# Eight-core transformer layer: three PSUM copies of the attention stage issued on ScalarE instead of VectorE

## The chip, the cores and the metric

One Trainium2 chip, 8 cores. Each core computes one batch element (2048 tokens of width 1024) of the same program; nothing is exchanged between cores. The metric is the device time of the slowest core in microseconds. The lines named L... are lines of the kernel file.

## The reference, cut to what matters

```python
x = x + 0.5 * ffn(layernorm(x))      # attention with 8 heads, 8 experts a head, top-2 gates
x = x + lightnet(layernorm(x))       # the stage that is changed
x = x + 0.5 * ffn(layernorm(x))

def lightnet(x):                     # T 2048, H 8 heads of 128
    q = silu(x @ Wq.T); k = x @ Wk.T; v = x @ Wv.T
    z = cumlogsumexp(k, axis=1)      # running over the tokens
    k = exp(k - z); g = shifted(z) - z
    # per token: S = exp(g) * S + k (x) v ;  o = q . S * 128**-0.5
    gate = x @ Wg1.T @ Wg2.T
    o = o * rsqrt(mean(o * o) + EPS) * g_norm_weight
    return (o * gate * sigmoid(gate)) @ Wo.T
```

## The kernel before

The program has three stages one after the other, each with a layer norm ahead of it: the feed-forward block, the recurrent attention ("GLA", `emit_gla`), and the feed-forward block again. Every instruction is put on an engine's stream by a helper that works out, from the buffers read and written, which semaphore counts it must wait for. Each engine runs its own stream strictly in the order in which the generators below emitted it, so that an instruction which waits holds up everything behind it on its engine. Weights come in 256 KB pieces over two staging slots and are cast by POOL.

In `emit_gla` the 8 heads are taken in 4 pairs, head A as s = 0 and head B as s = 1. For a pair:

- `proj_q(s, h, qtr)` projects one quarter (512 tokens) of one head: 8 matmuls for Q into bank 4 + s, Silu on ACT (L578); 8 for K into the same bank, a copy on DVE (L587); 8 for V into the same bank, a copy to SBUF (L597), 4 transposes on PE (L605) into the bf16 bank `PBB[s]`, and a copy of these to `VHB(s)` (L609).
- `fe_gen(s, h, qtr)` turns K and Q of the quarter into their decayed forms: Exp on ACT (L617), a cast on DVE (L620), a running sum on DVE (L627), a carry copy (L630), Ln and Exp on ACT (L633, L636), a multiply on DVE (L641). `fe_pair` does it for both heads, step by step in turn. PE can go on with the next chunk only when L641 is done.
- `chunk(s, h, c)` does 128 tokens of the recurrence with small 128 x 128 matmuls, two DVE operations (L662, L683) and two ACT Identity operations, L670 (out of `PBB[s]`) and L688.

The order for a pair: `proj_q` of quarters 0 and 1 for both heads, `fe_pair(0)`, chunks 0 to 3, `fe_pair(1)`, chunks 4 to 7 with the two `proj_q` of quarter 2 woven in one step a round and what is left of them after chunk 7 (`drain_bg`), `fe_pair(2)`, chunks 8 to 11 with quarter 3 in the same way, `fe_pair(3)`, chunks 12 to 15. Of the two woven projections head A's ends within the chunks; head B's V part comes in the drain. So three times in each pair (fe of quarters 0, 2 and 3) a V projection with its two copies stands right ahead of `fe_pair` in the streams, and once (quarter 1) a chunk does.

After the pairs comes the output part, in 4 groups of 512 tokens. A group has for each head a Square on ACT (L796, two buffers in `EXPT`) and a matmul of it that sums the squares, and after each of these one `wo_job` of the group before: 8 matmuls, a copy to `CTXH` (L766), 4 transposes (L773), an add to X on DVE (L781). Then the gate (L819 to L832) without any `wo_job` beside it. The last group's 8 jobs run by themselves.

Of the kernel before, what the change touches and what calls it, by code (L numbers as in the profile page):

```python
# [8 lines left out]
AF = mybir.ActivationFunctionType  # L9
# [90 lines left out]
def arnk(c0, c1):  # L100
    return [("ARN", b) for b in range(c0 // 512, cdiv(c1, 512))]
# [10 lines left out]
def ctxk(c0, c1):  # L112
    return [("CTXH", b) for b in range(c0 // 128, cdiv(c1, 128))]
# [6 lines left out]
def mm(kb, out_ap, lhsT_ap, rhs_ap, start, stop, reads, writes):  # L120
    kb.op("pe", lambda eo, o=out_ap, l=lhsT_ap, r=rhs_ap, s=start, p=stop:
          eo.matmul(o, l, r, start=s, stop=p, skip_group_check=True),  # L122
          reads=reads, writes=writes)
# [380 lines left out]
def emit_gla(kb, B, din, ld):  # L504
# [5 lines left out]
    X, SCR, SC2, EXPT, CTXH, GNW, STG = (B["X"], B["SCR"], B["SC2"], B["EXPT"],  # L510
                                         B["CTXH"], B["GNW"], B["STG"])
# [19 lines left out]
    def QHB(s):  return QH[:, s * 1024:(s + 1) * 1024]  # L531
    def KFB(s):  return U1[:, s * 1024:(s + 1) * 1024]
    def VHB(s):  return VH[:, s * 1024:(s + 1) * 1024]
# [13 lines left out]
    for g in range(4):  # L547
        bank = PSB[g % 2]
# [11 lines left out]
    def proj_q(s, h, qtr):  # L560
        base = (h % 2) * 4096
        rwa = ("WA", h % 2)
        slot = qtr % 2
        bq = ("QH2", s, slot)
        bk = ("U12", s, slot)
        bv = ("VH2", s, slot)
        t512 = qtr
        rx = [RXN[4 * t512 + j] for j in range(4)]
        bank = PSB[4 + s]
        rb = ("PSB", 4 + s)  # L570
        for dc in range(ND):
            mm(kb, bank[:, :],
               WA[:, base + dc * 128: base + (dc + 1) * 128],
               XN[:, dc * T + t512 * 512: dc * T + (t512 + 1) * 512],
               dc == 0, dc == ND - 1, reads=rx + [rwa], writes=[rb])
            yield
        kb.op("act", lambda eo, o=QHB(s)[:, slot * 512:(slot + 1) * 512], a=bank[:, :]:
              eo.activation(o, a, AF.Silu), reads=[rb], writes=[bq])  # L578
        yield
        for dc in range(ND):  # L580
            mm(kb, bank[:, :],
               WA[:, base + 1024 + dc * 128: base + 1024 + (dc + 1) * 128],
               XN[:, dc * T + t512 * 512: dc * T + (t512 + 1) * 512],
               dc == 0, dc == ND - 1, reads=rx + [rwa], writes=[rb])
            yield
        kb.op("dve", lambda eo, o=KFB(s)[:, slot * 512:(slot + 1) * 512], a=bank[:, :]:
              eo.tensor_copy(o, a), reads=[rb], writes=[bk])  # L587
        yield
        for dc in range(ND):
            mm(kb, bank[:, :],  # L590
               WA[:, base + 2048 + dc * 128: base + 2048 + (dc + 1) * 128],
               XN[:, dc * T + t512 * 512: dc * T + (t512 + 1) * 512],
               dc == 0, dc == ND - 1, reads=rx + [rwa], writes=[rb])
            yield
        vstg = GOTM[:, s * 512:(s + 1) * 512]
        rvs = ("GOTM", s)
        kb.op("dve", lambda eo, o=vstg, a=bank[:, :]: eo.tensor_copy(o, a),  # L597
              reads=[rb], writes=[rvs])
        yield
        pbv = PBB[s]  # L600
        rpbv = ("PBB", s)
        for tl in range(4):
            kb.op("pe", lambda eo, o=pbv[:, tl * 128:(tl + 1) * 128],
                  a=vstg[:, tl * 128:(tl + 1) * 128], idt=IDT[:, :]:
                  eo.transpose(o, a, idt),  # L605
                  reads=[rvs, ("IDT",)], writes=[rpbv])
            yield
        kb.op("dve", lambda eo, o=VHB(s)[:, slot * 512:(slot + 1) * 512],
              a=pbv[:, 0:512]: eo.tensor_copy(o, a),  # L609
              reads=[rpbv], writes=[bv])  # L610
        yield
    def fe_gen(s, h, qtr):
# [81 lines left out]
    for hp in range(4):  # L694
# [29 lines left out]
        for g0 in (proj_q(0, hA, 0), proj_q(1, hB, 0),  # L724
                   proj_q(0, hA, 1), proj_q(1, hB, 1)):
            for _ in g0:
                pass
# [3 lines left out]
        for c in range(NCH):  # L731
            run_pair(c)
            if c == 3:
                fe_pair(hA, hB, 1)
                bg.append(proj_q(0, hA, 2))
                bg.append(proj_q(1, hB, 2))
            if c == 7:
                drain_bg()
                fe_pair(hA, hB, 2)
                bg.append(proj_q(0, hA, 3))  # L740
                bg.append(proj_q(1, hB, 3))
            if c == 11:
                drain_bg()
                fe_pair(hA, hB, 3)
# [9 lines left out]
    def wo_job(dc, g):  # L754
        bank = PSB[2 + (dc % 2)]
        rb = ("PSB", 2 + (dc % 2))
        for hh in range(ND):
            mm(kb, bank[:, :],
               WB[:, hh * 1024 + dc * 128: hh * 1024 + (dc + 1) * 128],
               ARN[:, hh * T + g * 512: hh * T + (g + 1) * 512],  # L760
               hh == 0, hh == ND - 1,
               reads=arnk(hh * T + g * 512, hh * T + (g + 1) * 512) + [("WB",)],
               writes=[rb])
        cslot = dc % 2
        kb.op("dve", lambda eo, o=CTXH[:, cslot * 512:(cslot + 1) * 512],
              a=bank[:, :]: eo.tensor_copy(o, a),  # L766
              reads=[rb], writes=ctxk(cslot * 512, (cslot + 1) * 512))
        pb = PBB[dc % 2]
        rpb = ("PBB", dc % 2)
        for tl in range(4):  # L770
            kb.op("pe", lambda eo, o=pb[:, tl * 128:(tl + 1) * 128],
                  a=CTXH[:, cslot * 512 + tl * 128: cslot * 512 + (tl + 1) * 128],
                  idt=IDT[:, :]: eo.transpose(o, a, idt),  # L773
                  reads=ctxk(cslot * 512, (cslot + 1) * 512) + [("IDT",)],
                  writes=[rpb])

        def xadd(eo, pb=pb, g=g, dc=dc):
            src_ = pb[:, 0:512].rearrange("p (q c) -> p q c", q=4)
            dstv = B["X"].ap().rearrange("p (i d) -> p i d", i=NT)[
                :, g * 4:(g + 1) * 4, dc * 128:(dc + 1) * 128]  # L780
            return eo.tensor_tensor(dstv, dstv, src_, ALU.add)  # L781
        kb.op("dve", xadd,
              reads=[rpb] + [("X", g * 4 + tl) for tl in range(4)],
              writes=[("X", g * 4 + tl) for tl in range(4)])

    for g in range(4):
# [25 lines left out]
        for h in range(H):  # L812
            bank = PSB[h % 2]
# [25 lines left out]
        for dc in range(ND):  # L839
            wo_jobs.append(lambda dc=dc, g=g: wo_job(dc, g))  # L840
# [186 lines left out]
```

How the kernel before makes its waits and increments, by code:

```python
        def emit(eo, waits=tuple(waits), fn=fn, me=acct, st=step):  # L77
            for tgt, c in waits:
                eo.wait_ge(sems[tgt], c)
            fn(eo).then_inc(sems[me], st)
# [9 lines left out]
    def final_wait(self, eng, tgt):  # L90
        c = self.cnt[tgt]
        sems = self.sems
        self.streams[eng].append(lambda eo, t=tgt, c=c: eo.wait_ge(sems[t], c))
```

## Time and profile before

| | us |
|---|---|
| median of 3 runs | 4576.86 |
| lowest and highest of them | 4459.55, 4740.17 |
| the profiled execution | 4454.78 |
| its span on the slowest core | 4453.2 |

| engine | busy us | share of the span |
|---|---|---|
| PE | 3559.9 | 80% |
| DVE | 2120.9 | 48% |
| ACT | 963.5 | 22% |
| POOL | 402.2 | 9% |

The profile is of one execution, on the slowest core. The share of busy time is a mean over three stages; the changed lines are all in the middle one. "Idle before" is how long the engine stood still before an instruction, with what ended that.

### The profile page before, as it was taken

To read this page: it belongs to the slowest core of one execution; us is meant where nothing else is said; L and a number is where in the kernel's file an instruction comes from. 1 tells how busy PE (TensorE), PEld (TensorE's weight loads), DVE (VectorE), ACT (ScalarE), POOL (GpSimd) and SP (SyncE) were. 2 spreads that over 40 slices of the span, in tenths; PEclk is the share of its full clock that TensorE was granted. 3 is DMA by queue.
4 is the path that set the end of the run, shared out by engine and by line. 5 is a ranking of instruction groups with operands and counts; after the bars stand their busy time and mean duration, and the time that the engine had idled before them with its cause. 6 is when DMAs were issued, how large, how long until landed. Compare 5 with 4: busy or idle time off the path is not lost.

```text
span 4453.2 us, 54125 instructions; the slowest of 8 cores (4437.7 to 4453.2 us)
## 1 busy us (share of the span) xinstructions
PE 3559.9 (80%) x15409; PEld 1463.1 (33%) x15712; DVE 2120.9 (48%) x4892; ACT 963.5 (22%) x1731; POOL 402.2 (9%) x652
## 2 busy tenths in 40 slices
PE   2589899998989898654655543698989898989989
PEld 1234333333334343321222112233334343333333
DVE  4545453535354554532334455735354544536353
ACT  2021203031211212232233212030211212030302
POOL 1001010101010110001000010001010110101000
PEclk9689999999999999786777775899999999999999
DMA  5011111202021111001000011012021111111111
GB/s 152 29 34 53 34 53 38 62 24 81 19 67 41 46 53 29 1 12 55 29 24 1 1 52 43 16 33 79 17 72 36 50 53 34 53 34 57 34 34 76
DMA packets 142096, 190.35 MB, mean 43 GB/s; under 512 B 11624, under 2 KB 69096, under 8 KB 141808
## 3 DMA queue, kind: packets, MB, share of 16 engines
q1 hardware_dynamic: 99456, 106.98, 8.1%
q10 hardware_dynamic: 42352, 79.90, 5.8%
q8 instruction: 136, 2.23, 0.2%
q14 instruction: 152, 1.25, 0.1%
HBM read 178.44 MB, written 8.39 MB: 42 GB/s over the span
## 4 chain that ended last, share of the span: by engine, by line
PE 62%; DVE 22%; issue 8%; ACT 3%; DMA 2%; DVEq 1%; POOL 0%; SPq 0%; ACTq 0%; POOLq 0%
PE psp L122 40%; PE psb L122 20%; DVE SCR L379 10%; DVE SCR L375 1%; DVEq L79 1%; DMA STG<-fo 1%; DVE ARN L451 1%; DVE VH L382 1%; DVE SCR L198 1%; DVE SCR L196 1%; ACT ARN L223 1%; PE pbb L230 1%; DVE CTXH L766 1%; DVE GOTM L597 1%; DVE U L587 1%
## 5 line engine op out<-in xcount | busy, mean ns | idle before, releaser
L122 PE MATMUL psp<-WB,ARN 128*128 128x512 bf16 x4004 | 943.0, 380 | 25.5 <-DVE ARN L451 19.6
L407 ACT ACTIVATE EXPT<-psp 128x512 bf16<-128x512 f32 x704 | 415.0, 597 | 2289.2 <-PE psp L122 2195.3
L469 DVE SCALAR_TENSOR_TENSOR X<-psp,X 128x512 f32<-128x512 f32 x512 | 353.5, 690 | 421.0 <-PE psp L122 420.9
L122 PEld LDWEIGHTS psp<-WB,ARN 128*128 128x128 bf16 x4096 | 371.6, 98 | 500.7 <-issue 100.0
L122 PE MATMUL psb<-WA,XN 128*128 128x512 bf16 x2006 | 481.4, 385 | 57.6 <-DVE SCR L379 54.3
L122 PE MATMUL psp<-WA,XN 128*128 128x512 bf16 x2004 | 479.9, 384 | 44.1 <-DVE SCR L379 40.3
L435 DVE TENSOR_TENSOR CTXH<-psb,SC 128x512 bf16<-128x512 f32 x64 | 44.3, 692 | 816.2 <-PE psp L122 603.2
L122 PE MATMUL psp<-QH,KH 128*128 128x512 bf16 x1004 | 401.0, 416 | 8.7 <-DVE X L469 5.9
L379 DVE SCALAR_TENSOR_TENSOR SCR<-psp,GTM,SCR 128x128 f32<-128x128 f32 x896 | 314.0, 350 | 105.0 <-DVE SCR L379 13.1
L379 DVE SCALAR_TENSOR_TENSOR SCR<-psb,GTM,SCR 128x128 f32<-128x128 f32 x896 | 313.9, 350 | 104.3 <-DVE SCR L379 18.6
L122 PE MATMUL psb<-EXPT,VH 128*128 128x512 bf16 x692 | 282.2, 408 | 90.4 <-DVE SCR L379 81.8
L451 DVE TENSOR_TENSOR ARN<-CTXH,psp 128x512 bf16<-128x512 bf16 x512 | 342.2, 678 | 13.6 <-PE psp L122 10.5
L142 POOL CAST WB<-STG 128x512 bf16<-128x512 f32 x272 | 168.1, 618 | 1807.9 <-PE psp L122 1424.4
L142 POOL CAST WA<-STG 128x512 bf16<-128x512 f32 x304 | 189.2, 622 | 1538.6 <-PE psb L122 1161.5
L122 PE MATMUL psb<-EXPT,ONESB 128*128 128x512 bf16 x713 | 292.3, 410 | 16.3 <-ACT EXPT L796 15.4
L122 PEld LDWEIGHTS psb<-WA,XN 128*128 128x128 bf16 x2048 | 191.5, 98 | 337.9 <-issue 140.4
L122 PE MATMUL psb<-XN,WA 128*128 128x512 bf16 x741 | 223.7, 430 | 95.4 <-ACT QH L578 63.9
L122 PEld LDWEIGHTS psp<-WA,XN 128*128 128x128 bf16 x2048 | 191.6, 98 | 323.2 <-issue 124.2
L122 PE MATMUL psp<-GFMH,SELE 8*128 8x512 bf16 x512 | 212.4, 420 | 58.1 <-DVE ARN L451 55.3
L122 PE MATMUL psp<-XN,QKW 128*128 128x512 bf16 x1031 | 252.6, 403 | 4.6 <-ACT SCR L257 2.7
L407 ACT ACTIVATE CTXH<-psp 128x512 bf16<-128x512 f32 x320 | 191.2, 598 | 32.6 <-PE psp L122 21.3
L230 PE MATMUL pbb<-IDT,ARN 128*128 128x128 bf16 x384 | 48.5, 306 | 152.4 <-ACT ARN L223 150.1
(109 smaller groups left out, 2502.9 us busy)
## 6 DMA issues: line engine op xcount, KB each, us to landing
STG<-fv SPq DMA_DIRECT2D x256, 256.0 KB, 2.7
STG<-fo ACTq DMA_DIRECT2D x256, 256.0 KB, 2.8
X<-x SPq DMA_DIRECT2D x16, 512.0 KB, 14.7
STG<-fq_t SPq DMA_DIRECT2D x32, 256.0 KB, 2.7
STG<-fk_t SPq DMA_DIRECT2D x32, 256.0 KB, 2.7
y<-X ACTq DMA_DIRECT2D x16, 512.0 KB, 4.1
STG<-wq_t SPq DMA_DIRECT2D x16, 256.0 KB, 2.9
STG<-wk_t SPq DMA_DIRECT2D x16, 256.0 KB, 2.9
```

The source lines that it names most:

```text
L79: eo.wait_ge(sems[tgt], c)
L122: eo.matmul(o, l, r, start=s, stop=p, skip_group_check=True),
L142: self.kb.op("gp", lambda eo, d=dstf, s=stg: eo.tensor_copy(d(), s), reads=[skey], writes=list(wkeys))
L196: kb.op("dve", lambda eo, o=SCR[:, 0:6], a=xt[:, 0:512]: eo.bn_stats(o, a), reads=[rX], writes=scrk(0, 128))
L198: kb.op("dve", lambda eo, o=SCR[:, 6:12], a=xt[:, 512:1024]: eo.bn_stats(o, a), reads=[rX], writes=scrk(0, 128))
L223: eo.activation(o, a, AF.Identity, bias=b, scale=s),
L230: eo.transpose(o, a, idt),
L375: eo.tensor_scalar(o, a, g, None, ALU.mult),
L379: eo.scalar_tensor_tensor(o, a, g, c, ALU.mult, ALU.add),
L407: eo.activation(o, i_, AF.Exp, scale=SCALE_FFN),
L451: eo.tensor_tensor(o, a, b, ALU.mult),
L469: eo.scalar_tensor_tensor(o, a, 0.5, x, ALU.mult, ALU.add),
```

## The change

The copies at L597, L609 and L766 are issued on ACT as Identity activations instead of on DVE as tensor copies. Sources, destinations, the position in the emission order and the buffers are as before. Each line is executed 32 times in a program.

```diff
         vstg = GOTM[:, s * 512:(s + 1) * 512]
         rvs = ("GOTM", s)
-        kb.op("dve", lambda eo, o=vstg, a=bank[:, :]: eo.tensor_copy(o, a),
+        kb.op("act", lambda eo, o=vstg, a=bank[:, :]:
+              eo.activation(o, a, AF.Identity),
               reads=[rb], writes=[rvs])
...
-        kb.op("dve", lambda eo, o=VHB(s)[:, slot * 512:(slot + 1) * 512],
-              a=pbv[:, 0:512]: eo.tensor_copy(o, a),
+        kb.op("act", lambda eo, o=VHB(s)[:, slot * 512:(slot + 1) * 512],
+              a=pbv[:, 0:512]: eo.activation(o, a, AF.Identity),
               reads=[rpbv], writes=[bv])
...
         cslot = dc % 2
-        kb.op("dve", lambda eo, o=CTXH[:, cslot * 512:(cslot + 1) * 512],
-              a=bank[:, :]: eo.tensor_copy(o, a),
+        kb.op("act", lambda eo, o=CTXH[:, cslot * 512:(cslot + 1) * 512],
+              a=bank[:, :]: eo.activation(o, a, AF.Identity),
               reads=[rb], writes=ctxk(cslot * 512, (cslot + 1) * 512))
```

## Rows read from the trace of the kernel before

**Rows 1.** The page: busy time by engine, and the chain that ended last.

```profile
PE 3559.9 (80%) x15409; PEld 1463.1 (33%) x15712; DVE 2120.9 (48%) x4892; ACT 963.5 (22%) x1731; POOL 402.2 (9%) x652
...
PE 62%; DVE 22%; issue 8%; ACT 3%; DMA 2%; DVEq 1%; POOL 0%; SPq 0%; ACTq 0%; POOLq 0%
```

**Rows 2.** Stretches, first head pair and output part: length; busy, count by engine; clock.

```profile
1889.00:2050.00 161.00, 78.06 (x403) 35.80 (x409) 50.96 (x125) 42.06 (x104) 18.47 (x28) 0.77 0.15 43
...
2449.00:2680.00 231.00, 108.08 (x444) 40.43 (x453) 125.20 (x201) 52.50 (x82) 13.55 (x22) 0.71 0.09 25
```

**Rows 3.** DVE groups by line and form: busy us, mean ns | idle before.

```profile
L766 DVE CAST CTXH<-psp 128x512 bf16<-128x512 f32 x32 | 22.1, 691 | 47.2 <-PE psp L122 47.2
L597 DVE CAST GOTM<-psb 128x512 bf16<-128x512 f32 x32 | 22.1, 690 | 56.4 <-PE psb L122 56.4
...
L609 DVE COPY VH<-pbb 128x512 bf16<-128x512 bf16 x32 | 13.6, 424 | 24.4 <-PE pbb L605 23.5 <-PE psb L122 1.0
```

**Rows 4.** ACT groups by line and form.

```profile
L670 ACT ACTIVATE CTXH<-pbb 128x128 bf16<-128x128 bf16 x128 | 28.5, 275 | 92.5 <-PE pbb L666 78.0 <-PE pbb L605 14.6
...
L578 ACT ACTIVATE QH<-psb 128x512 bf16<-128x512 f32 x32 | 19.1, 597 | 120.5 <-PE psb L122 120.3
...
L578 ACT ACT_TABLE_LOAD x12 | 15.4, 1283 | 53.8 <-DMA STG<-wo_t 26.8 <-PE psb L122 24.9 <-PE psp L122 2.1
L617 ACT ACT_TABLE_LOAD x12 | 15.4, 1283 | 0.2
```

**Rows 5.** Who waited for L597 and for L766: us in total, times.

```profile
  PE pbb L605: 26.3, 32
```

```profile
  PE pbb L773: 30.4, 32
```

**Rows 6.** Timeline, first pair, ahead of fe of quarter 2: start, us, instruction.

```profile
1967.10 0.60 ACT L578 ACTIVATE QH<-psb 128x512 bf16<-128x512 f32 x1 [1.45 <-PE psb L122]
1967.72 1.28 ACT L617 ACT_TABLE_LOAD   x1
...
1970.67 1.89 PE L122 MATMUL psb<-XN,WA 128*128 128x512 bf16 x8 [0.94 <-DVE U L587]
1972.67 0.69 DVE L597 CAST GOTM<-psb 128x512 bf16<-128x512 f32 x1 [2.14 <-PE psb L122]
...
1973.51 0.38 PE L605 MATMUL pbb<-IDT,GOTM 128*128 128x128 bf16 x4 [0.94 <-DVE GOTM L597]
1974.00 0.42 DVE L609 COPY VH<-pbb 128x512 bf16<-128x512 bf16 x1 [0.64 <-PE pbb L605]
...
1975.00 2.45 DVE L627 TENSOR_TENSOR_SCAN U<-ONESF,LNS,U 128x512 f32<-128x512 f32 x2
...
1980.20 0.27 PE L122 MATMUL psp<-QH,EXPT 128*128 128x128 bf16 x1 [6.31 <-DVE QH L641]
```

**Rows 7.** Timeline, first pair, fe of quarter 1, behind chunk 3.

```profile
1943.04 1.15 ACT L617 ACTIVATE U<-U 128x512 f32<-128x512 f32 x2
...
1944.63 2.45 DVE L627 TENSOR_TENSOR_SCAN U<-ONESF,LNS,U 128x512 f32<-128x512 f32 x2
```

**Rows 8.** Timeline, output part: group 0 without jobs, then a job of group 1.

```profile
2451.19 1.15 ACT L796 ACTIVATE EXPT<-ARN 128x512 bf16<-128x512 bf16 x2 [0.30 <-PE psp L122]
...
2451.96 1.10 PE L122 MATMUL psb<-EXPT,ONESB 128*128 128x512 bf16 x2 [0.35 <-ACT EXPT L796]
...
2488.18 0.69 DVE L766 CAST CTXH<-psp 128x512 bf16<-128x512 f32 x1 [1.25 <-PE psp L122]
...
2489.24 0.38 PE L122 MATMUL psb<-EXPT,ONESB 128*128 128x512 bf16 x1
```

**Rows 9.** Stretches as in rows 2, after two gaps of PE; then from the timeline.

```profile
1980.20:1987.70 7.50, 4.79 (x19) 2.31 (x21) 2.16 (x7) 2.77 (x6) 0.00 (x0) 0.58 0.00 1
...
2049.20:2062.00 12.80, 10.86 (x28) 3.48 (x28) 1.81 (x3) 0.00 (x0) 0.62 (x1) 0.52 0.14 41
...
2049.25 3.57 PE L122 MATMUL psb<-XN,WA 128*128 128x512 bf16 x8 [25.65 <-ACT QH L578]
```

## The prediction, before the result was known

> **What bounds the kernel now.** I read the page first: PE is busy for 80% of the span and makes 62% of the chain that ended last, DVE for 48% and 22% of the chain, ACT for 22% [rows 1]. Over the whole program ACT looks like the place with room. But all three edited lines are in the middle stage, so the shares that count are that stage's. By stretches, in the first head pair PE is busy 78 of 161 us, DVE 51, ACT 42; in the output part PE 108 of 231 us, DVE 125, ACT 52 [rows 2]. No engine is full there: the stage is bound by latency, by one engine waiting for the next. So what a move is worth is not busy time taken off DVE, but how the path from one PE instruction to the next changes. The groups by line give the durations [rows 3, 4], the waiters give what PE stands still for [rows 5], and the timeline gives the order at the three kinds of place where the copies stand [rows 6 to 8].
>
> **What the change does to each copy.** The DVE copy of a 128x512 f32 bank takes 690 ns, and ACT's Silu of the same shape out of the same bank 597 [rows 3, 4]. An Identity is not in the trace at this size; I take 597, so -0.093 us for L597 and L766. The bounds are 0.275 us (the Identity of a quarter of the size, L670) and 0.690 us (no better than DVE); the Silu row is the nearest, same size, source and type. L609 reads bf16, where DVE needs only 424 ns [rows 3]; on ACT I take 597 again, +0.173 us, bounded by 0.275 and 0.690 in the same way. The Trainium skill ("ScalarE: Activation LUTs", Rules for kernel authors) says to keep plain arithmetic on VectorE, up to about 3 times faster there in bf16. For the f32 banks the two rows above speak the other way, for L609 with it. If it held for all three in the measure of L609's row (+0.173 for 96 copies), the change would cost 17 us by that alone, wherever a copy is waited for.
>
> PE waited 26.3 us for L597 (32 times 0.82) and 30.4 us for L766 (32 times 0.95) [rows 5]. So all that faster copies could give back is 0.093 of each 0.69 in there, 64 x 0.093 = 6 us.
>
> **Does an Identity bring table loads?** Loads stand 12 times before a Silu and 12 times before the Exp of L617 [rows 4], which is three switches each way in each of 4 pairs. Between them the 128 Identities of L670 run with whichever table is there, and have no load in the groups. So no loads are added; their number stays at 24. What counts is where they stand.
>
> **The place that pays: the copies ahead of fe (12 times).** In the kernel before, ACT's stream is Silu, table load, Exp, Exp: after the last Silu at 1967.10 the load starts at 1967.72, under PE's K and V matmuls, and both Exps are done before V is [rows 6]. When V ends at 1972.56 (1970.67 + 1.89), DVE has L597 and L609, and the running sum starts at 1975.00, 2.44 us after V's end. The change puts both copies into ACT's stream ahead of that table load, and ACT can't pass them. What is queued behind the waiting copy is just what was hidden: the load and the two Exps. From V's end, with the waits of [rows 6]: 0.11 to the copy, 0.60 copy, 0.15 to PE, 0.38 transposes, 0.11 to the second copy, 0.60 copy: 1.95 us. Then 0.02 + 1.28 for the load: 3.26. From the start of the Exp pair to the start of the running sum take the place where nothing hides it, quarter 1: 1944.63 - 1943.04 = 1.59 us [rows 7]. That makes 4.85 us against 2.44: +2.41 us. Behind it everything is a serial chain to PE, which already stands still for 6.31 us there [rows 6], so nothing takes it up. Three such places in a pair (fe of quarters 0, 2, 3), 4 pairs: 12 x 2.41 = +28.9 us. Quarter 1's fe stands behind chunk 3 on ACT and does not change.
>
> The load itself is 1283 ns, and the Exp follows at once: 1967.72 + 1.28 is 1969.00, with the next activation in the trace. The Trainium skill ("ScalarE: Activation LUTs", What ACT_TABLE_LOAD costs) counts a drain of about 1380 ns with each switch, which this trace does not show beside these loads. By the page's figure the 12 places would cost 12 x 1.38 = 16.6 us more, and the whole would be 48 instead of 31.5.
>
> **The other V copies.** The 12 remaining of the prologues (3 in each pair) have only the next projection behind them: L609 is long done when the next Silu is due. They give 12 x -0.093 = -1.1 us. The 8 of head A woven into the chunks have chunk work of ACT (L670, L688) behind them; PE waits for L597 to transpose, so -0.09 each, and the longer L609 delays L688, which PE doesn't wait for in that round: 8 x -0.09 = -0.7 us.
>
> **The output part.** In a job DVE's copy starts at 2488.18 and PE's next sum-of-squares matmul at 2489.24, 1.06 us later; its Square was made during the job's matmuls, since ACT ran two ahead [rows 8]. Moved to ACT, the copy stands between one Square and the next, so the next Square waits for the 8 matmuls and the copy. From the copy's start: about 0.50 to the Square's start (two activations of 0.63 take 1.15 together, so they overlap by 0.1), and 2451.96 - 2451.19 = 0.77 from a Square's start to its matmul [rows 8]: 1.27 against 1.06, +0.21 us. That holds for 7 jobs in each of 3 groups: 21 x 0.21 = +4.4 us. The other 11 (the last of each group and the final 8) give 11 x -0.09 = -1.0 us.
>
> **The clock.** After PE's gap of 6.31 us ahead of fe the granted clock is 0.58 on the mean of 7.5 us: mostly the lower of the two levels (1.2 of 2.4 GHz) [rows 9]. The longer gap only lengthens time in which PE is idle. After the longest gap of the stage, 25.65 us, the lower level lasted for about 12.8 us, at 0.52 on the mean, and 8 large matmuls took 3.57 us there against 1.89 at the upper level, 0.21 more each [rows 6, 9]. If each of the 4 gaps ahead of chunks 8 to 11 became like that one, some 5 us more at the lower level with about 14 large matmuls would be 2.9 us each, 12 us. The lower bound is 0 (it is at the lower level anyway). I take +1. Ahead of chunks 0 and 12 no large matmuls follow.
>
> **Sum.** 28.9 - 1.1 - 0.7 + 4.4 - 1.0 + 1.0 = +31.5 us. On the profiled execution that gives 4454.78 + 31.5 = 4486.3 us (1.6 us of it outside the span). That execution is 2.7% below the median of the runs shown, 4576.86, and just under their lowest, 4459.55. The change adds waits and leaves the rest alone, so I add the same to the median: 4608 us, a ratio of 1.007.
>
> **The rivals.**
> - *The table load stays hidden* (12%): the load would be made ahead of the copies, since an Identity runs with either table. Against it: each load in the trace stands directly ahead of the activation that needs it, behind the previous one's wait [rows 6]. 12 x 1.28 less: +16 us, 4593.
> - *A drain with each exposed switch* (10%): the mechanism is that ACT must empty between the copy and the load, which in the hidden places might go unseen. The Silu's end at 1967.70 and the load at 1967.72 speak against it [rows 6]. +48 us, 4625. The page named above is for it.
> - *The clock tips* (4%), the case on the slow side: PE, with gaps of 8.7 instead of 6.3 us, stays at the lower level in the projections too. Each large matmul costs 0.21 us more, and there are 768 projection matmuls and 256 in the jobs. It decides (2% is 92 us) from about 60 / 0.21 = 290 of them on. All of them would give at most 1024 x 0.21 = 215 us more, 4823. Against it: the prologues run at full clock between gaps of 0.9 us, and these hardly change.
> - *The waits for the copies go away* (4%): DVE would have been late for other work, and with the copies gone PE no longer waits. At most 26.3 + 30.4 = 57 us less [rows 5], 4520, still within 2%. Against it: DVE was idle ahead of nearly each of them, for PE [rows 3].
>
> The forecast itself has 70%. Its own range is +20 to +45 us.
>
> **How the numbers follow.** A measurement of this kernel tells about 2% from no change. Faster by over 2% needs more than the last rival's full bound: 2%. Slower by over 2% is the clock's case and some unknown: 5%. The rest, 93%, is within. The low end of the range is the hidden load on the profiled execution's own time, 4454.78 + 15 = 4470, since the runs shown lie both near it and near their median. The high end is the median with the drain and the clock's bound: 4576.86 + 48 + 12 = 4637, say 4640.
>
> **What would show it.** In the profile after: L597, L609, L766 on ACT with about 597 ns each, ACT table loads still 24 in the stage, all 12 of L617 behind L609 with no cover. PE's gap ahead of fe of quarters 0, 2 and 3 goes from 6.3 to about 8.7 us, that of quarter 1 stays. The running sum starts about 4.85 us after V's last matmul. In the output part Square starts after the copy, and PE waits for it. I am wrong if the Exps of L617 are done before V's copies, if an Identity gets a table load of its own, or if the first pair, from its first projection to the second pair's, does not grow by 6 to 8 us.

## The result and the profile after

| | before | changed |
|---|---|---|
| median of 28 runs each, us | 4461.47 | 4487.79 |
| lowest | 4456.94 | 4482.77 |

The ratio is 1.0054 (95% interval 1.0042 to 1.0065), so the change costs about 24 us. That is less than 2%, but the interval lies clear of 1. In some executions the four cores of one die get a lower TensorE clock and are some per cent longer, whatever the kernel: the ratio leaves these out, the first median of three (4576.86) was such a run, and in the profiled executions of the changed kernel and of the one with the earlier Exps below only the four undisturbed cores are read (cores 0 to 3 and 4 to 7).

The rows of the changed kernel come from core 2 (4476.9 us, clock 0.896; the same core before: 4451.8). The slowest core is 24 to 26 us later, the mean of the cores 28 (4448.3 before, 4476.4 after), because the cores of the kernel before lie further apart.

First the groups of ACT in the middle stage, after; columns as in [rows 4]:

```profile
L598 ACT ACTIVATE GOTM<-psb 128x512 bf16<-128x512 f32 x32 | 19.1, 597 | 128.2 <-PE psb L122 128.2
L610 ACT ACTIVATE VH<-pbb 128x512 bf16<-128x512 bf16 x32 | 19.1, 597 | 17.1 <-PE pbb L606 17.0
...
L767 ACT ACTIVATE CTXH<-psp 128x512 bf16<-128x512 f32 x32 | 19.1, 597 | 84.6 <-PE psp L122 84.6
...
L578 ACT ACT_TABLE_LOAD x12 | 15.4, 1283 | 49.5 <-POOL WB L142 26.5 <-PE psb L122 20.1 <-PE psp L122 2.9
L618 ACT ACT_TABLE_LOAD x12 | 15.4, 1283 | 0.2
```

All three copies take 597 ns, and the loads are 12 and 12 as in [rows 4]: an Identity brings none. (From L597 on, the line numbers of the changed kernel are one to two higher.) Then the place ahead of fe of quarter 2 in the first pair, which answers to [rows 6]:

```profile
1973.68 1.89 PE L122 MATMUL psb<-XN,WA 128*128 128x512 bf16 x8 [0.94 <-DVE U L587]
1975.67 0.60 ACT L598 ACTIVATE GOTM<-psb 128x512 bf16<-128x512 f32 x1 [4.96 <-PE psb L122]
1976.41 0.38 PE L606 MATMUL pbb<-IDT,GOTM 128*128 128x128 bf16 x4 [0.84 <-ACT GOTM L598]
1976.89 0.60 ACT L610 ACTIVATE VH<-pbb 128x512 bf16<-128x512 bf16 x1 [0.62 <-PE pbb L606]
1977.50 1.28 ACT L618 ACT_TABLE_LOAD   x1
1978.80 1.15 ACT L618 ACTIVATE U<-U 128x512 f32<-128x512 f32 x2
...
1980.39 2.45 DVE L628 TENSOR_TENSOR_SCAN U<-ONESF,LNS,U 128x512 f32<-128x512 f32 x2
...
1985.59 0.27 PE L122 MATMUL psp<-QH,EXPT 128*128 128x128 bf16 x1 [8.80 <-DVE QH L642]
```

V ends at 1973.68 + 1.89 = 1975.57. The table load that ran under PE's matmuls in [rows 6] now starts 1.93 us behind that, the running sum 4.82 us (2.44 before), and PE's gap is 8.80 us where it was 6.31. Nothing on PE overlaps the load or the Exps any more. The waits of PE that changed in the middle stage, core 2, before and then after (us in total, times, longest):

```profile
PE psp L122 <- DVE QH L641: 110.6, 28, 7.4
...
PE psb L122 <- DVE U L587: 27.1, 32, 1.3
PE pbb L605 <- DVE GOTM L597: 26.6, 32, 0.9
```

```profile
PE psp L122 <- DVE QH L642: 139.2, 28, 9.6
...
PE psb L122 <- DVE U L587: 28.9, 32, 1.1
PE pbb L606 <- ACT GOTM L598: 23.2, 32, 0.8
```

29 us more in the wait for the last instruction of fe, 3 us less in the wait for the V copy. Place by place on core 2, PE's gap ahead of fe goes from 6.2 to 8.7 us in quarter 0, from 6.3 to 8.8 in quarter 2 and from 6.6 to 7.4 up to 8.8 to 9.6 in quarter 3, and stays near 6.9 in quarter 1. To compare kernels below, the middle stage is cut by starts in the timelines: the head pairs (first Silu of L578 to the first Silu of the gate) and the output part (from there to the Ln of the next layer norm). The values are means over the cores of one execution each. "PE waits" sums the time within the pairs in which PE stands still for another engine; the rest is PE at work or between its own instructions, and it moves with the clock.

| | head pairs | of it PE waits | rest | output part |
|---|---|---|---|---|
| before | 558.0 | 248.8 | 309 | 230.4 |
| changed | 587.0 | 275.5 | 312 | 229.3 |

The cores of the kernel before spread from 550.8 to 564.0 us in the pairs, in steps of some 3 us, all with nearly the same waits (247.6 to 250.0). The steps are in the rest, and a few us in this table are no finding.

### The profile page after: what moved, and what is told of

Its sections match the earlier page's. It is cut to its first block, busy times and chain, and to the rows that moved or that the text cites. A ratio compares the mean times of both kernels' runs of the same rounds, so it can differ in the third digit from the quotient of the medians.

```text
span 4570.6 us, 54470 instructions; the slowest of 8 cores (4475.8 to 4570.6 us)
## 1 busy us (share of the span) xinstructions
PE 3717.5 (81%) x15712; PEld 1500.6 (33%) x15712; DVE 2065.8 (45%) x4796; ACT 1017.9 (22%) x1827; POOL 402.0 (9%) x652
## 4 chain that ended last, share of the span: by engine, by line
PE 68%; DVE 17%; issue 7%; ACT 5%; DMA 2%; DVEq 1%; POOL 0%; SPq 0%; ACTq 0%; POOLq 0%
PE psp L122 43%; PE psb L122 23%; DVE SCR L379 7%; DVEq L79 1%; DVE ARN L451 1%; DVE SCR L375 1%; DMA STG<-fo 1%; DVE SCR L198 1%; DVE SCR L196 1%; ACT ARN L223 1%; DVE VH L382 1%; PE pbb L230 1%; DVE U L587 0%; DMA X<-x 0%; DVE SC L827 0%
## 5 line engine op out<-in xcount | busy, mean ns | idle before, releaser
L122 PE MATMUL psp<-WB,ARN 128*128 128x512 bf16 x4096 | 1000.6, 394 | 19.4 <-DVE ARN L451 19.4
L122 PEld LDWEIGHTS psp<-WB,ARN 128*128 128x128 bf16 x4096 | 381.1, 100 | 534.8 <-issue 234.3
L122 PE MATMUL psb<-WA,XN 128*128 128x512 bf16 x2048 | 507.4, 400 | 43.1 <-DVE SCR L379 43.0
L122 PE MATMUL psp<-WA,XN 128*128 128x512 bf16 x2048 | 507.6, 400 | 31.8 <-DVE SCR L379 31.6
L122 PE MATMUL psp<-QH,KH 128*128 128x512 bf16 x1024 | 416.6, 426 | 4.9 <-DVE X L469 4.9
L122 PE MATMUL psb<-EXPT,VH 128*128 128x512 bf16 x704 | 294.3, 418 | 72.3 <-DVE SCR L379 65.1
L122 PE MATMUL psb<-EXPT,ONESB 128*128 128x512 bf16 x736 | 307.3, 418 | 16.3 <-ACT EXPT L797 15.1
L122 PE MATMUL psb<-XN,WA 128*128 128x512 bf16 x768 | 235.1, 436 | 91.3 <-ACT QH L578 62.6
L122 PE MATMUL psp<-XN,QKW 128*128 128x512 bf16 x1056 | 269.5, 420 | 2.1 <-ACT SCR L257 2.1
L230 PE MATMUL pbb<-IDT,ARN 128*128 128x128 bf16 x384 | 48.5, 306 | 153.8 <-ACT ARN L223 151.7
```

## The experiments

**The V copies alone, and the output copy alone.** The change was cut in two: L597 and L609 on ACT (as in the diff above), or L766 alone. "Theory A" in the expectations is the prediction's account: the copies on ACT hold up the table load and the Exps behind them.

> The two V copies (L597, L609) on ACT, the output part's copy (L766) left on DVE. Theory A (the table load and the two Exps of L617 lose their cover): the time from the first Silu of the first head pair to the first Silu of the output part grows by 26 to 30 us on the mean of the cores, and PE's wait for L641 from 110 to about 139 us, as in the changed kernel; the whole +27 us. Rival B (it is the move as a whole, DVE or the clock, that costs): less than 20 us of it. The output part, 230.4 us before and 229.3 after: if the earlier rise of the clock in it comes from the later start of the part, it is shorter here, near 225 us; if it comes from the jobs' own changed order, it stays 230.4.

> Only L766 on ACT. The head pairs stay at 558 us on the mean of the cores. By the prediction's sum (each Square behind the copy, +0.21 us for 21 jobs, 0.09 off for 11) the output part goes from 230.4 to 233.8 us and the whole is +3.4 us. By the trace of the changed kernel the job period goes from 3.27 to 3.46 us, but TensorE's clock rises one job earlier in each group: then the output part is 229.3 us and the whole -1. If that rise came from the shift of 29 us ahead of it, the part is about 234 us here. PE's transposes of the first job take 0.58 us if the clock is still low then, 0.38 if not.

| | ratio to before | head pairs | PE waits | output part |
|---|---|---|---|---|
| V copies only | 1.0052 (1.0037 to 1.0067) | 590.5 | 275.7 | 228.6 |
| L766 only | 0.9996 (0.9984 to 1.0009) | 564.1 | 249.9 | 230.3 |

The V copies carry the whole loss; PE's wait for L641 was 138.7 us on the mean of the cores, as expected, and the pairs grew by 32.5 us, 27 of them in the waits, where 26 to 30 were expected. L766 on ACT changes nothing that can be measured in the whole. Its head pairs, whose code is that of the kernel before, came out 6 us longer in this execution with 1 us more of waits: that is the size of what one execution can tell. On the output part neither of the two simple answers held. The jobs, by the starts of PE's first two groups of transposes, before (core 2) and then in the changed kernel (core 2):

```profile
2479.03 0.59 PE L773 MATMUL pbb<-IDT,CTXH 128*128 128x128 bf16 x4 [0.94 <-DVE CTXH L766]
...
2484.31 0.38 PE L773 MATMUL pbb<-IDT,CTXH 128*128 128x128 bf16 x4 [0.94 <-DVE CTXH L766]
...
2487.58 0.38 PE L773 MATMUL pbb<-IDT,CTXH 128*128 128x128 bf16 x4 [0.94 <-DVE CTXH L766]
```

```profile
2502.27 0.60 ACT L767 ACTIVATE CTXH<-psp 128x512 bf16<-128x512 f32 x1 [4.12 <-PE psp L122]
2502.76 0.62 ACT L797 ACTIVATE EXPT<-ARN 128x512 bf16<-128x512 bf16 x1
2503.01 0.38 PE L774 MATMUL pbb<-IDT,CTXH 128*128 128x128 bf16 x4 [0.84 <-ACT CTXH L767]
...
2506.47 0.38 PE L774 MATMUL pbb<-IDT,CTXH 128*128 128x128 bf16 x4 [0.84 <-ACT CTXH L767]
```

The Square (L797) now starts right behind the copy, half a microsecond after it, and the period of a job goes from 3.27 to 3.46 us: +0.19, the step that was forecast as +0.21. But four transposes take 0.59 us at the lower clock level and 0.38 at the upper, and in the changed kernel the first ones already take 0.38: the clock has risen one job earlier. The distance to the second is 3.46 us where it was 5.28. In the kernel before the rise came late in all of the first 3 groups, in the changed one early in all 3 (cores 0 to 3 alike). With the V copies alone it came early in group 1 only, on all cores. With L766 alone the cores differ: early in all 3 groups on cores 4 and 5 (part 228.2 us), in groups 2 and 3 on five cores (230.6 to 230.9), in group 2 only on core 1 (231.9). An early rise is worth 1.8 us with the copy on DVE (V copies alone: 230.4 to 228.6 with one) and 1.1 to 2.6 with the copy on ACT. So the 3 early rises gave back what the Squares cost. Neither the later start nor the new order of a job alone sets when it comes; what does is open.

**One V copy at a time.**

> Only the first V copy (L597) on ACT. Theory A (what counts is how long ACT's table load and Exps are held up behind V's end): the load starts 0.73 us after V's last matmul, the running sum 0.73 + 1.28 + 1.59 = 3.60 us after it against 2.44 before, so 12 x 1.16 - 20 x 0.09 = +12 us, PE's wait for L641 from 110 to about 125. A rival that counts moved copies by their length (ACT 0.09 us shorter) expects -3 us, since this is the copy that got faster.

> Only the second V copy (L609) on ACT. Theory A: the load waits for the transposes and this copy, the running sum starts 4.94 us after V's last matmul, 12 x 2.5 = +30 us, PE's wait for L641 near 140: the full loss of the changed kernel from one copy of the two, so that the losses of the two single moves (12 and 30) don't add up to that of both (28). The rival by length expects at most 12 x 0.17 = +2 us.

| | result | wait for L641, mean | head pairs | PE waits |
|---|---|---|---|---|
| L597 only | 1.0040 (1.0024 to 1.0056) | 123.9 | 580.4 | 262.8 |
| L609 only | lowest run 4486.16 against 4458.88 | 139.4 | 590.9 | 279.4 |

L609 alone brings the full loss, +27 us by the lowest runs (there is no interval for it); its waits grew by 31 us, where 30 were expected. L597 alone brings +18 us, where 12 were expected: the waits grew by 14 us, and the rest by 8 us (318 against 309), at a mean clock of 0.745 in place of 0.765. The copy that became shorter by 0.09 us costs 14 us of waits, and the losses of the two don't add up. A count by the length of the copies is refuted; what counts is where the load and the Exps stand. The place with L609 alone:

```profile
1975.36 0.69 DVE L597 CAST GOTM<-psb 128x512 bf16<-128x512 f32 x1 [2.14 <-PE psb L122]
1976.19 0.38 PE L605 MATMUL pbb<-IDT,GOTM 128*128 128x128 bf16 x4 [0.94 <-DVE GOTM L597]
1976.67 0.60 ACT L609 ACTIVATE VH<-pbb 128x512 bf16<-128x512 bf16 x1 [6.28 <-PE pbb L605]
1977.29 1.28 ACT L617 ACT_TABLE_LOAD   x1
```

ACT had been idle for 6.28 us ahead of that copy. It could have done the load and both Exps in that time, had its stream not put the copy first.

**The table loads taken away.** In both kernels Q's Silu is an Identity, so that one table serves the head pairs; Q is then not what the reference wants.

```diff
-              eo.activation(o, a, AF.Silu), reads=[rb], writes=[bq])
+              eo.activation(o, a, AF.Identity), reads=[rb], writes=[bq])
```

> The kernel before with the Silu of Q (L578) replaced by an Identity, which changes the result: ACT keeps one table through the head pairs, so 24 loads are gone. Theory A: the 12 loads ahead of L578 were in PE's way, the 12 ahead of L617 were under PE's matmuls, so the head pairs lose 12 x 1.28 = 15 us. If a drain of over 1 us went with each load, they lose 30 or more.

> The changed kernel with the same replacement (it changes the result). Theory A: both kinds of load are in the way here, so it loses 24 x 1.28 = 31 us against the changed kernel, and stands 13 us above the kernel before with the replacement, where the changed kernel stands 28 us above the kernel before: half of the loss is the load, the other half the two Exps and the order. A drain with each exposed load would make it 48 us or more against the changed kernel.

| | ratio to before | head pairs | PE waits | wait for L578 | wait for L641 |
|---|---|---|---|---|---|
| before | | 558.0 | 248.8 | 63.6 | 109.6 |
| before, one table | 0.9925 (0.9896 to 0.9953) | 533.8 | 233.9 | 48.2 | 109.7 |
| changed | 1.0054 | 587.0 | 275.5 | 63.0 | 138.8 |
| changed, one table | 0.9946 (0.9929 to 0.9963) | 543.4 | 242.3 | 48.3 | 121.5 |

By the waits the expectation holds well: 15 us less in the kernel before, all of it at L578 (15.4, 12 x 1.283), none at L641, so the loads of L617 were hidden there; 33 us less in the changed one (31 expected), 14.7 of it at L578 and 17.3 at L641. The times moved more, 33 and 48 us, and by themselves they would meet the sign that the expectations gave for a drain (30 or more, 48 or more). The rest of the pairs shrank too, by 9 and 10 us, at a mean clock of 0.779 and 0.776 in place of 0.765 and 0.754, and the other 5 to 9 us lie outside the pairs. So the drain has to be judged by the waits and the rows. The waits are 15.4 / 12 = 1.28 us a load at L578 in the kernel before, and 1.44 at L641 in the changed one. In the rows of both kernels (core 2) every load of L617 starts 0.02 us behind the activation before it, 11 of the 12 of L578 start 0.08 us behind PE's last projection matmul (a Silu without a load 0.10; the twelfth stands behind the wo_t loads in ACT's stream), and all 24 have their activation 0.01 us behind them. That leaves no room for a drain of 1.38 us. Between the two kernels with one table 9 us are left (pairs 9.6, waits 8.4, expected 13; the two intervals overlap), which is the Exps and the order.

**The Exps put back under the matmuls.** The Exp of L617 of quarters 0, 2 and 3 is emitted by `proj_q` of head B right after its K copy, and `fe_gen` keeps that of quarter 1 alone; once in the changed kernel, once as a control in the kernel before. From the edit:

```diff
               eo.tensor_copy(o, a), reads=[rb], writes=[bk])
         yield
+        if s == 1 and qtr != 0:
+            for s2 in (0, 1):
+                emit_k_exp(s2, 0 if qtr == 1 else qtr)
```

> The changed kernel with the Exp of L617 of quarters 0, 2 and 3 emitted for both heads right after head B's K copy, ahead of head B's V copies. Theory A: ACT does the table load and the Exps under the K and V matmuls again, and since DVE now has no V copy in its stream, its cast and running sum start during the V matmuls: about 1.4 us after V's first matmul starts instead of 4.33 in the kernel before and 6.7 in the changed one. So 12 x 2.9 = 35 us less than before, 64 less than the changed kernel; 4459 - 36 = 4423 us, ratio 0.992. Rival B (the V copies on ACT cost by themselves): still slower than before.

> Control: the same earlier emission of the Exp, with all three copies on DVE. The Exps were already done early there, and DVE's cast stands behind L609 in its stream as before, so theory A expects no change, within 0.1%. If this one gains as well, the gain of the other is the emission's alone and not the copies' place.

With the V copies on ACT: ratio 0.9932 (0.9906 to 0.9957), about 30 us faster than before and 54 faster than the changed kernel. The ratio rests on two runs of this kernel; by the lowest runs it is 39 us (4417.90 against 4457.31) and 65, and 35 and 64 were expected. Head pairs 520.8 us, PE waits 208.3. The control: 1.0001 (0.9990 to 1.0012). The same copies on the same engine are a loss or a gain, by what stands behind them. The first such place, ahead of fe of quarter 0, in the kernel before (core 2) and then in this one (core 4):

```profile
1936.10 0.27 PE L122 MATMUL psp<-QH,EXPT 128*128 128x128 bf16 x1 [6.20 <-DVE QH L641]
```

```profile
1920.99 1.28 ACT L564 ACT_TABLE_LOAD   x1
1921.12 1.89 PE L122 MATMUL psb<-XN,WA 128*128 128x512 bf16 x8 [0.84 <-ACT QH L585]
1922.29 1.15 ACT L564 ACTIVATE U<-U 128x512 f32<-128x512 f32 x2
...
1923.95 1.89 PE L122 MATMUL psb<-XN,WA 128*128 128x512 bf16 x8 [0.94 <-DVE U L594]
1924.39 2.33 DVE L638 TENSOR_TENSOR_SCAN U<-ONESF,U 128x512 f32<-128x512 f32 x2
1925.93 0.60 ACT L608 ACTIVATE GOTM<-psb 128x512 bf16<-128x512 f32 x1 [2.50 <-PE psb L122]
...
1930.25 0.22 PE L122 MATMUL psp<-QH,EXPT 128*128 128x128 bf16 x1 [3.19 <-DVE QH L652]
```

The running sum starts 0.44 us after V's first matmul, under PE's work, and PE's gap is 3.19 us where it was 6.20.

**Is the move needed for that?** In the next kernel all copies stay on DVE, and Exp, cast, running sum and carry are emitted ahead of the V copies (`emit_k_sum` runs the first half of `fe_gen` for both heads, and `fe_pair` then the second half alone). The other one adds to the fast version a Square emitted one job earlier.

```diff
+        if s == 1 and qtr != 0:
+            emit_k_sum(0 if qtr == 1 else qtr)
```

```diff
+        emit_sq(0)
         for hh in range(H):
+            if hh + 1 < H:
+                emit_sq(hh + 1)
             mm(kb, sq[:, :], ONESB[:, :], sqb, hh == 0, hh == H - 1, ...)
```

> The kernel before, all copies on DVE, with the first half of fe (Exp, cast, running sum, carry, of quarters 0, 2 and 3) emitted for both heads after head B's K copy, ahead of head B's V copies. DVE then has 3.4 us of work ahead of L597, which comes about 1.4 us late after V's end, but the Ln of L633 starts behind the carry and not behind V. Theory: as with the copies on ACT, the running sum no longer stands behind the V copies, and PE goes on about 6.5 us after V's first matmul starts in both; so about as fast as that one, 30 to 38 us below before. If DVE's extra work in front of the V copy counts in full, it gains 12 x 1.4 = 17 us less.

> The changed kernel with the earlier Exps and, in the output part, each Square emitted one job earlier, so that it is made under the job's matmuls again while the copy L766 stays on ACT. The job period should fall from 3.46 to 3.18 us (before: 3.27, copy 0.09 shorter), 21 x 0.28 = 6 us less than the version with the earlier Exps alone, at most 2 us a group more or less by where the clock rises. About 4425 us where that one had about 4430.

| | ratio to before | head pairs | PE waits | wait for L641 | wait for L597 | output part |
|---|---|---|---|---|---|---|
| all on DVE, sum first | 0.9907 (0.9864 to 0.9950) | 524.3 | 207.2 | 48.5 | 45.8 | 230.2 |
| copies on ACT, Exp and Square first | 0.9890 (0.9851 to 0.9930) | 522.0 | 208.2 | 71.1 | 23.8 | 231.7 |

Both are as fast as the version before them within their intervals. With everything on DVE the V copies come late, as expected, and PE waits 19 us more for them than in the kernel before, but 61 us less for L641, which gives the same sum. By the lowest runs the three versions with the earlier start of fe are 39, 44 and 41 us faster than the kernel before. So the gain of about 40 us comes from emitting the start of fe ahead of the V copies, and which engine makes the copies makes no difference that these runs can tell. The earlier Squares brought the period of a job to 3.28 us, not to the 3.18 that were expected: PE's transposes start about 0.1 us later behind the copy from the third job on. The trace shows what is different there. In the first two jobs of each group they wait for one semaphore, ACT's, and start 0.14 us after the copy's end; in all 24 later jobs (core 2) they wait for two, ACT's for the copy and DVE's, and start 0.26 us after it (0.43 in one job a group). With the copy on DVE it was one semaphore for all of them, and 0.15 us. So the move to ACT has a small price of its own here, which took up the 0.09 us of the shorter copy. The output part did not get shorter (231.7 against 231.4): the clock rose late in 2 of its first 3 groups (in 1 of them with the earlier Exps alone) and in the last group one job later still.

## Why the prediction was right in its mechanism and wrong in its time

- **Durations.** 597 ns for an Identity of a 512-column bank was taken from Silu's row and is exact for all three lines. The rule of the Trainium skill ("ScalarE: Activation LUTs", Rules for kernel authors) sends `add`, `mul` and the like to VectorE and names no copies. Carried over to these copies, it would be wrong for the two f32 banks (690 ns on DVE, 597 on ACT) and right for the bf16 one (424 against 597).
- **No added loads; the load exposed 12 times.** Right. +2.41 us a place were forecast, 2.38 measured at the place shown; 28.9 us in all against 29.2 more in the wait for L641. That the place of the load and the Exps does it, and not the copies' length or DVE, was tested by moving each copy alone, by taking the loads away and by moving the Exps. The loads stay 24 in the head pairs; the 24 "in the stage" of the prediction left out 7 in the output part (L808, L819), the same number in both kernels. The first pair grew by 8.5 us on the mean of the cores (127.7 to 136.2), slightly more than the 6 to 8 that the prediction had set as its test.
- **The rivals.** The load did not stay hidden: it starts 1.93 us behind V. The waits for the copies did not go away: 26.6 to 23.2 us and 30.2 to 29.8 on core 2. The clock did not tip: the rest of the pairs grew by 2 us.
- **A drain with each switch** (the rival with 48 us). Refuted by the waits and the rows: 1.28 us of wait a load, at most 0.08 us ahead of a load that had nothing else to wait for, and 0.01 us behind it. The measurement decides against the figure of the Trainium skill ("ScalarE: Activation LUTs", What ACT_TABLE_LOAD costs) for loads like these, where ACT has just gone idle or does one activation after the other.
- **The other V copies.** -1.8 us forecast; PE's wait for the V copy fell by 3.3 us, of which the 12 ahead of fe are in the term above.
- **The output part.** The step (+0.21 us for 21 jobs) was +0.19, the term +3.4 us; the part came out at -1.1, since the clock rose one job earlier three times. The 0.09 us that the last 8 jobs were to gain did not come either: their period is 3.05 us before and 3.06 after. This is the term that the sum had wrong, by 4.5 us: the prediction put the clock of the output part at nothing and gave no reason. It weighed the clock for the head pairs only.
- **The clock in the pairs.** +1 us taken, bounded by 12; the rest of the pairs grew by 2 us, well inside the spread of the cores.
- **The sum and where it was put.** +31.5 us forecast; 24 by the ratio, 26 by the medians and 28 on the mean of the cores measured, within its own range of +20 to +45. The step that failed is the last one, "I add the same to the median": it takes the median of three runs, 4576.86, for the level of this kernel, and gives 4608 where 4487.79 was measured. Of these 121 us, 115 are the level (28 runs of the kernel before have their median at 4461.47) and 5 are the sum. Two readings spoke against that level at the time: the profiled execution took 4454.78 us, and the lowest of the three, 4459.55, agreed with it to 0.1%, while the other two lay 117 and 281 us above it, apart from each other too. Where two executions agree and the others scatter upward, the sum belongs on the two. Put on the profiled execution it gave 4486.3 us, 1.5 from the measured median, but part of that is luck: this execution lies 7 us below the median of 28, and the sum was 5 us too large. The measured time lies inside the range that was given, 4470 to 4640, but near its low end, for the same reason. The forecast of "within 2%" was right and too coarse: the loss of 0.5% is clear of the noise of 28 runs.

## What to carry to other kernels

When work is moved to an engine with room, look at what stands behind it in that engine's stream, not at its busy share: an instruction that waits for PE holds up every later one, and the table load and the first step of the next phase are the ones that had been running early at no cost. Move such a copy only together with what is to run ahead of it, and try first whether the earlier emission alone is the gain. A term of a few us a stage can be undone by the clock of TensorE rising one burst earlier or later, so compare several kernels and several cores before explaining it. And put a forecast change on a level that at least two executions agree on, not on a median of three that lie far apart.

## What was not expected of the hardware

The time in which PE is at its lower clock level moves with small shifts of the work. PE's waits in the head pairs account for 27 of the 29 us of the changed kernel, but only for 14 of 22 us with L597 alone, and for 15 of 24 with the loads taken away from the kernel before. In the output part the rise came in the first job of a group or in the second (in the last group of two kernels in the third), worth 1.1 to 2.6 us each time, differently in kernels whose jobs differ by 0.2 us, and with L766 alone differently on the cores of one execution of one kernel. What decides this was not found.

An instruction of PE that waits for two semaphores started 0.12 us later behind the copy than one that waits for one (0.26 against 0.14 us, in the jobs of the kernel with the earlier Squares).
